# Distance attention: a pair's product, copy, turning back and output moved apart, the logarithm without a bias, copies of values one head later

## The reference, cut to what matters

```python
scores = einsum('bhid,bhjd->bhij', qh, kh) / sqrt(DH)
p = softmax(where(maskb, scores, -1e32)) * maskb
cum, tot = cumsum(p, axis=-1), sum(p, axis=-1, keepdims=True)
pos = abs(idx[None, :] - idx[:, None])
dist_scores = sqrt(clip((tot - cum) * pos, 0.0, None))
gamma, diff = -softplus(gammas), exp(sigmoid(pdiff))
total_effect = clip(exp(dist_scores * gamma * diff), 1e-5, 1e5)
scores = softmax(where(maskb, scores * total_effect, -1e32))
out = einsum('bhij,bhjd->bhid', scores.at[:, :, 0, :].set(0.0), vh)
```

## Time and profile before

| | us |
|---|---|
| median of 3 runs | 3448.16 |
| lowest, highest | 3440.13, 3451.22 |
| profiled execution | 3469.66 |
| its span | 3467.7 |
| outside the span | 2.0 |
| distance attention, first scores to last output | 2549 to 3367 |
| PE, DVE, ACT, POOL busy over the whole span | 81%, 57%, 50%, 23% |

### The profile page before, as it was taken

How to read it: one execution, slowest core, us unless ns; L and a number is a source line. 1 busy time by engine, 2 the same in 40 slices (tenths; PEclk the granted TensorE clock), 3 DMA queues, 4 the chain that set the end, 5 groups by cost and what they waited for, 6 DMA issues and landing times. The chain is left out here.

```text
span 3467.7 us, 48835 instructions
## 1 busy us (share of the span) xinstructions
PE 2800.7 (81%) x14992; PEld 1568.3 (45%) x14992; DVE 1960.3 (57%) x4849; ACT 1729.6 (50%) x2836; POOL 803.8 (23%) x911
## 2 busy tenths in 40 slices
PE   4899849879999997666899769997657777777777
PEld 2333339734444454323322449995424434343443
DVE  6677631255555554027688501113678888888853
ACT  1366412146555553001477313331369898989953
POOL 2000020010000000002000120003257777777740
PEclk8899969989999998788799989998869999999998
DMA  4111136520000002872121329993410000000001
GB/s 157 37 52 52 46 124 227 179 73 1 1 1 1 1 1 121 353 318 95 46 61 58 131 98 345 345 346 107 153 19 19 19 15 18 24 18 9 25 22 52
DMA packets 160959, 326.54 MB, mean 94 GB/s; under 512 B 29360, under 2 KB 128432, under 8 KB 137136
## 3 DMA queue, kind: packets, MB, share of 16 engines
q1 hardware_dynamic: 156208, 312.13, 25.7%
q0 software_dynamic: 4608, 12.59, 1.1%
HBM read 275.22 MB, written 49.28 MB: 94 GB/s over the span
## 5 line engine op out<-in xcount | busy, mean ns | idle before, releaser
L3133 DVE TENSOR_TENSOR_SCAN L3x_fade<-L3x_first_exp,L3x_scores 128x513 f32<-128x513 f32 x256 | 311.5, 1217 | 47.2 <-PE L3x_probs_tp L2943 46.2
L3014 POOL TENSOR_TENSOR L3x_fade<-L3x_fade,L3x_apart 128x1024 f32<-128x1024 f32 x128 | 278.9, 2179 | 195.0 <-DVE L3x_mx L3151 157.2
L2940 PE MATMUL L3x_probs_tp<-identity,L3x_fade 128*128 128x128 f32 x1024 | 162.6, 282 | 176.5 <-ACT L3x_probs_T L3079 144.4
L1430 ACT ACTIVATE L1x_probs<-L1x_scores,L1x_neg_max 128x512 f32<-128x512 f32 x256 | 173.5, 683 | 226.6 <-DVE L1x_neg_max L1484 226.6
L2940 PEld LDWEIGHTS L3x_probs_tp<-identity,L3x_fade 128*128 128x128 f32 x1024 | 113.1, 141 | 282.4 <-issue 141.4
L1484 DVE TENSOR_REDUCE L1x_neg_max<-L1x_scores 128x2 f32<-128x1024 f32 x128 | 156.7, 1224 | 142.9 <-PE L1x_scores L1319 142.9
L1824 ACT ACTIVATE L2f_hiddenT<-L2f_hidden_ps,L2f_b1s 128x128 f32<-128x128 f32 x320 | 99.9, 363 | 208.8 <-PE L2f_hidden_ps L1759 208.8
L3051 ACT ACTIVATE L3x_first_exp<-L3x_scores,L3x_nm 128x512 f32<-128x512 f32 x256 | 175.4, 685 | 53.9 <-DVE L3x_nm L3125 52.1
L930 DVE CUSTOM_DVE_ANT_0 L0x_masked_scores<-L0x_s,L0x_mask_q 128x512 f32<-128x512 f32 x256 | 167.1, 686 | 57.3 <-issue 57.1
L3059 ACT ACTIVATE L3x_fade<-L3x_fade,L3x_tiny,L3x_rl 128x512 f32<-128x512 f32 x256 | 194.4, 814 | 0.0
L925 DVE TENSOR_REDUCE L2x_neg_max<-L2x_s 128x1 f32<-128x512 f32 x256 | 164.7, 686 | 39.6 <-PE L2x_s L819 39.1
(11 more groups left out here) (522 smaller groups left out, 6080.8 us busy)
## 6 DMA issues: line engine op xcount, KB each, us to landing
L2f_w1s<-in_L_w SPq DMA_DIRECT2D x40, 1024.0 KB, 7.7
L2f_w2s<-in_L_w SPq DMA_DIRECT2D x40, 1024.0 KB, 6.4
L1f_w1s<-in_L_w SPq DMA_DIRECT2D x32, 1024.0 KB, 17.2
L1f_w2s<-in_L_w SPq DMA_DIRECT2D x32, 1024.0 KB, 10.6
L0f_w1s<-in_L_w SPq DMA_DIRECT2D x16, 1024.0 KB, 6.2
L0f_w2s<-in_L_w SPq DMA_DIRECT2D x16, 1024.0 KB, 5.2
L0x_q_stack<-L0x_q_parts SPq DMA_DIRECT2D x96, 64.0 KB, 2.4
L0x_k_stack<-L0x_k_parts SPq DMA_DIRECT2D x96, 64.0 KB, 2.5
```

Source lines behind the costliest of these rows:

```text
L1430: nc.scalar.activation(p[:, n % 3, h, :], s[:, n % 2, h, :], ACT.Exp, bias=nmax[:, n % 4, h:h + 1], accum_out=den[:, n % 4, h:h + 1]).then ...
L2940: nc.tensor.matmul(tp[:, kt, :], fz[:, f, kt * P:(kt + 1) * P], c.ident[:], start=(kt == 0), stop=False, is_transpose=True)
L3014: nc.gpsimd.tensor_tensor(fz[:, f:f + 2, 0:S], fz[:, f:f + 2, 0:S], w, ALU.mult).then_inc(y_done, 1)
L3133: nc.vector.tensor_tensor_scan(fz[:, f, :], ex[:, t, :], sA[:, t, 0:1].to_broadcast([P, S + 1]), 0.0, ALU.add, ALU.bypass).then_inc(f_done, 1)
```

## The change

- TensorE: `turn_back` of a pair leaves tile step 2 of the odd step and goes to tile step 0 of the even step behind it, after that step's first scores. `weigh` stays.
- ScalarE: `turned_copy` goes from tile step 1 to tile step 2 of the odd step, behind the last exponential and ahead of the root.
- VectorE: `outputs` goes from tile step 3 of the odd step to tile step 2 of the even step.
- GpSimd: `values` is done one head step later, at the same place in the body.
- The logarithm loses its bias operand `tiny` (1e-18). In its place the scan's leading column is set to 1e-18 in place of 0, once, and the host gives a distance of at least 1e-15. The memset of `tiny` goes.
- `run` goes one head step further (to U + 4 inclusive).

```diff
--- before.py
+++ after.py
@@ distance_attention
-        tiny = c.sb(ctx, tag + "tiny", [P, 1], F32)
...
@@ run
-            for k in range(56, U + 4):
+            for k in range(56, U + 5):
                 body(k, k % 8, k // 2)
@@ TensorE, body
-                        if i % 2 and there(k + (-4)):
-                            if t == 0:
-                                weigh(g + (-2), i // 2 % 2)
-                            elif t == 2:
-                                turn_back(g + (-2), i // 2 % 2)
+                        if i % 2 and t == 0 and there(k + (-4)):
+                            weigh(g + (-2), i // 2 % 2)
+                        if i % 2 == 0 and t == 0 and there(k + (-5)):
+                            turn_back(g + (-3), (i // 2 + 1) % 2)
@@ GpSimd, body
-                    if there(k + (-2)):
-                        values(k + (-2), (i - 2) % 8, g + (-1))
+                    if there(k + (-3)):
+                        values(k + (-3), (i - 3) % 8, g + (-1 if i % 2 else -2))
@@ ScalarE, log and body
-                        nc.scalar.activation(fz[:, f, 0:S], fz[:, f, 0:S], ACT.Ln, bias=tiny[:], scale=rl[:, f:f + 1]
+                        nc.scalar.activation(fz[:, f, 0:S], fz[:, f, 0:S], ACT.Ln, scale=rl[:, f:f + 1]
                                              ).then_inc(ln_done, 1)
...
-                        if t == 1 and i % 2 and there(k + (-4)):
+                        if t == 2 and i % 2 and there(k + (-4)):
                             turned_copy(g + (-2))
@@ VectorE, set-up and body
-                nc.vector.memset(ex[:, :, 0:1], 0.0)
-                nc.vector.memset(tiny[:], 1e-18).then_inc(cleared, 1)
+                nc.vector.memset(ex[:, :, 0:1], 1e-18).then_inc(cleared, 1)
...
-                        if t == 3 and i % 2 and there(k + (-4)):
-                            outputs(g + (-2))
+                        if t == 2 and i % 2 == 0 and there(k + (-5)):
+                            outputs(g + (-3))
@@ host_layout
-    d["distance"] = np.abs(at[:, None] - at[None, ::-1])
+    d["distance"] = np.maximum(np.abs(at[:, None] - at[None, ::-1]), np.float32(1e-15))
```

## The result

The changed kernel takes 3477.82 us in the median (3475.25 to 3489.60, 4 runs), the kernel before 3446.78 on the same chip: a ratio of 1.0094, 95% interval 1.0077 to 1.0110. It is slower by 0.94% by the ratio, and the medians lie 31.0 us apart. Forecast were 3459 us and a range that ended at 3470.

A forecast was written before the change was run, and what follows sets the result against it. A ring of waits, no full engine, was taken as the bound. Six rounds of 101.48 against 99.98 give +9.0, pairs outside the loop +2: +11, a median of 3459 us (+0.32%), range 3434 to 3470.

The forecast's parts named there:

- The path that was replayed: Exponential, turning, product, copy, logarithms, turning back, outputs, maximum, next exponential, then VectorE and the second head's clip; period 24.82 us before.
- both new costs: L3166 (now L3163) on VectorE blocked by GpSimd's product, 0.31 us; first scores waiting for late loads, making loaded pairs 25.51.
- two waits that the change removes: ScalarE's 1.10 us wait for the product before its copy, and VectorE's 0.83 for the turning back before the outputs.
- The clips: VectorE's clip, 1.32 us in the second head and 0.69 in the first; all in the loop to take about 0.69.
- Pairs without loads: Loop pairs with no group load due: 24.88 us apart, plus 0.70 per round of four pairs.
- the sum: Loop of 24 pairs: a round is 2 x 25.51 + 2 x 24.88 + 0.70 = 101.48 us, six rounds +9.0.
- it starts at 15.57, the outputs at 15.57 + 2.15 + 1.07 + 1.15: Loaded pairs: turning back, delayed by late loads, starts at 15.57; outputs at 19.94 us, period 25.51.
- rival (D): GpSimd's chain ends later than 19.72, L3166 waits up to 2.36 us; each 0.33 costs 10 us, beyond 3470 possible; chance 0.11.
- The period without the two costs: Pair period in the loop with L3166 not blocked and loads in time: 24.57 us.
- worth 0 in the new order: ScalarE's logarithm without bias saves 0.09 us x 4 a head, 23 us of work, but gains 0 because ScalarE waits anyway.
- the block's price: VectorE's small product L3166 ends at 19.72 rather than 19.41, 0.31 us later, making the period 24.88 rather than 24.57.
- The late loads' price: SyncE's loads land after first scores need them, delaying the turning back: loaded pairs 25.51 us in place of 24.88.

The follow-up runs named there:

- the fillings: Changed kernel plus five unused matmuls before the wait for a group's loads and six behind the even step's second scores: 3458.78 us, ratio 1.0042.
- mask_set_pair: Changed kernel with L3163 replaced by a written zero and loads in groups of two heads, started earlier: 3455.14 us, ratio 0.9954.
- pair_loads: Changed kernel with queries and keys loaded in groups of two heads in place of four, each started earlier: 3465.88 us, ratio 1.0057.
- before_all_but_moves: Kernel before with the logarithm without bias, the written zero for L3166 and early two-head loads, no step moved: 3437.26 us, ratio 0.9975.
- late_loads_before: Kernel before with four tiny extra transfers ahead of each group's loads, so these land later; nothing moved: 3465.91 us, ratio 1.0059.
- fill_gap: Changed kernel with early two-head loads, plus six unused matmuls behind the even head step's second scores: 3472.09 us, ratio 0.9996.

## Why the prediction was wrong

**Right.** The path that was replayed, and both new costs. The two waits that the change removes are gone and the period does not fall. L3163 is blocked until GpSimd's product ends. First scores wait for loads 14 times in the layer, 0.95 on average, and the turning back waits behind them. The clips take 0.69. Pairs without loads are at 24.87. With TensorE's clock held up, the loop is 1.2 us from the sum (607.64 against 608.88).

**The step that failed** is "it starts at 15.57, the outputs at 15.57 + 2.15 + 1.07 + 1.15", the term for the pairs with loads. It adds TensorE's wait and then takes TensorE's next steps at their old durations. They no longer have these when the clock has fallen to half: 2.15 becomes 4.1, and the waits of VectorE and ScalarE grow with it. The twelve pairs measured 26.80 in place of 25.51, 15.5 us more, where the loop is off by 14.8 (the pairs without loads take back 0.7: 25.17 against 25.23). In ratios: 1.0094 without and 1.0042 with the fillings. The clock's share is 0.5%, more than the 0.32% forecast for the whole change. In the loop the page of before could not show this, its clock being 1.00 there; but in other layers the same page has slices at 6 to 8 tenths, so a fall was to be reckoned with, and the sum lengthened an idle time of TensorE and never asked what its clock would do. Because no rival had it either, the range ended at 3470; rival (D) named another mechanism for its end, a later GpSimd, which did not come.

**A second place of the same kind** was not seen: the outputs in their new place, and the blocked product in them, hold not only the path but the maximum that second scores wait for. That wait was 0.2 in the mean before; it is 0.7 with the outputs moved and the product replaced (mask_set_pair), and 1.1 in the changed kernel and 1.5 in pair_loads with the product. At full clock the forecast had the periods right without it; together with the 1.37 behind it, it goes ahead of the fall in pair_loads, and its filling gives back 14.1 us of the loop (614.24 to 600.11).

**Sizes.** The period without the two costs was put at 24.57 and is 24.26 (582.33 / 24). Turning back came 2.60 behind the first exponential in mask_set_pair (2831.11 to 2833.71), not 2.75. The logarithms in between have no bias, which accounts for it by the size (0.18), though no run took that apart: the logarithm was said to be worth 0 in the new order, which holds only as long as the blocked product sets the period. So the block's price was too low: at full clock 600.11 - 582.33 = 17.8 us of the loop, where the sum of before gave (24.88 - 24.57) x 24 plus 4.2 for the rounds, 11.6. The late loads' price at full clock is 607.64 - 600.11 = 7.5, forecast 12 x 0.63 = 7.6. So the sum with both costs came out near by its path over GpSimd's product; the sum without them, and with it the price of the block, did not. Outside the loop the layer is +6.4 (214.7 to 221.1), forecast +2; the mean clock is some 0.8 in both kernels between the first scan and the loop, and this was not taken apart.

**Open** is why the clock falls in one loaded pair and not in the next: the length of the wait does not tell it. In the changed kernel a wait of 0.85 was followed by the fall (0.57 over 2652.5 to 2655), and one of 1.13 was not (1.00 from 3173 to 3179), and I have not found a rule in the rows:

```profile
2652.36 0.39 PE L2918 MATMUL L3x_scores<-L3x_k_stack,L3x_q_stack 96*128 96x512 bf16 x1 [0.85 <-DMA L3x_k_stack<-L3x_k_parts]
2652.50:2655.00 2.50, 2.50 (x14) 2.38 (x12) 1.56 (x6) 2.00 (x4) 2.50 (x2) 0.57 0.05 13
...
3173.78 0.39 PE L2918 MATMUL L3x_scores<-L3x_k_stack,L3x_q_stack 96*128 96x512 bf16 x1 [1.13 <-DMA L3x_k_stack<-L3x_k_parts]
3173.00:3179.00 6.00, 5.16 (x35) 3.85 (x37) 3.69 (x9) 4.21 (x7) 5.68 (x6) 1.00 0.00 0
```

The distribution over the pairs also differs from execution to execution, so a profile of one cannot price it to better than some us.

## What to carry to other kernels

When a new order makes TensorE wait, also in places that cost nothing on the path, read its granted clock and price its next steps at both levels; here the lower level cost 16.1 us of the loop (623.73 - 607.64), beside 25.3 for the two new waits at full clock (607.64 - 582.33). Before steps are moved, look at what each small one shares with what will run beside it: with one product of 128x8 elements and one late group of loads the changed order is 0.9% slower than the kernel before, with both repaired 0.5% faster. About half of that gain, 0.25%, the repairs and the logarithm bring without any step moved (before_all_but_moves).

## What the runs showed of the hardware

- TensorE's clock fell from 1.00 to 0.50 although no wait of TensorE in the loop of pair_loads is longer than 2.0 us: two waits of 1.3 and 1.4 us with 0.6 us of matmuls between them came before it (2681.4 to 2684.7). The wait alone did not decide it: in late_loads_before one of 1.16 us left the clock at 1.00 and its pair at 24.93 us, against 24.92 without the wait.
- Six unused matmuls (1.46 us) in one such place a pair held the mean clock at 1.00 over 600 us, with one fall, and made the loop 14.1 us shorter (fill_gap against pair_loads).
- A VectorE product of 128x8 elements from two SBUF tiles takes 0.17 us, and up to 1.32 beside a GpSimd product (changed kernel); a write of zero to the same tile takes 0.06 in all 32 places, also beside one (mask_set_pair).
